# One matrix per system in place of attention and inverse, factors stored with the systems, and other groups of tiles

## What is computed

```
A0   = tril(-(k_beta @ k.T) * L, -1)
A    = inverse(eye - A0)                 # unit lower triangular, 37 x 37
v_new = A @ (v * beta)
attn = tril((k @ k.T) * L)               # diagonal included
o    = attn @ v_new
out  = h + o @ W_read.T
```

## Time and profile before

| | |
|---|---|
| median of 3 runs | 774.7 us (774.45 to 776.15) |
| the profiled execution | 774.87 us, span 773.1 us |
| TensorE busy | 691.6 us (89%) |
| VectorE busy | 419.6 us (54%) |
| ScalarE busy | 246.4 us (32%) |
| GpSimd busy | 292.1 us (38%) |
| mean granted TensorE clock | 0.945 |

### The profile page before, as it was taken

One profiled execution on the slowest core, in us unless ns is written; L12 is line 12 of the kernel. 1 busy time (PEld: TensorE's weight loads), 2 busy tenths in 40 slices (PEclk: granted clock), 3 DMA queues, 4 the chain that ended last, 5 costly groups with the idle time before them and its releaser, 6 DMA issues.

```text
span 773.1 us, 13815 instructions
## 1 busy us (share of the span) xinstructions
PE 691.6 (89%) x4632; PEld 518.9 (67%) x4632; DVE 419.6 (54%) x1120; ACT 246.4 (32%) x679; POOL 292.1 (38%) x483
## 2 busy tenths in 40 slices
PE   5899999999997689999999689497999999999994
PEld 3567776676765445999998567374667676766763
DVE  2466677777665466334389999457233323333331
ACT  0122333333333114344444246261122223232231
POOL 2334454544444100255576687360222322222221
PEclk9899999999998779999999899796799999999998
DMA  8311001111100000000101327598211111111110
GB/s 292 137 37 37 20 25 31 37 37 37 37 1 2 1 1 2 1 8 6 40 8 36 41 44 290 210 361 306 56 40 43 49 54 47 58 42 56 47 35 14
DMA packets 25070, 50.73 MB, mean 66 GB/s; under 512 B 15611, under 2 KB 15741, under 8 KB 24363
## 3 DMA queue, kind: packets, MB, share of 16 engines
q1 hardware_dynamic: 21387, 35.36, 14.4%
q0 software_dynamic: 3328, 10.23, 4.4%
q10 hardware_dynamic: 288, 4.27, 1.4%
HBM read 39.99 MB, written 9.86 MB: 64 GB/s over the span
## 4 chain that ended last, share of the span: by engine, by line
PE 45%; DVE 7%; issue 4%; POOL 3%; ACT 0%; POOLq 0%; DVEq 0%; ACTq 0%
PE psum L1199 12%; PE psum L1175 12%; PE psum L1396 4%; PE psum L1408 4%; PE psum L1188 3%; PE psum L1442 2%; DVE work L1750 2%; PE psum L1376 1%; DVE arena_w L1757 1%; PE psum L1386 1%; PE psum L1018 1%; PE psum L1418 1%; POOL work L1909 1%; PE psum L1448 1%; POOL work L1898 1%
## 5 line engine op out<-in xcount | busy, mean ns | idle before, releaser
L1272 ACT ACTIVATE work<-psum,cst 128x128 f32<-128x128 f32 x208 | 56.5, 383 | 144.2 <-PE psum L1188 144.2
L1175 PE MATMUL psum<-arena_w,work 128*128 x208 | 93.7, 593 | 1.0 <-DVE work L1226 1.0
L1199 PE MATMUL psum<-arena_w,work 128*128 x416 | 94.2, 379 | 0.4 <-ACT work L1272 0.4
L1137 POOL DMA_INDIRECT out<-work,row_i x26 | 25.7, 988 | 158.2 <-DVE work L1248 158.2
L1199 PEld LDWEIGHTS psum<-arena_w,work 128*128 128x128 f32 x416 | 77.1, 190 | 10.5 <-issue 1.1
L1235 DVE COPY work<-psum 128x512 f32<-128x512 f32 x52 | 36.0, 692 | 67.5 <-PE psum L1175 67.5
L347 PE MATMUL psum<-arena_w 128*111 128x256 f32 x264 | 63.3, 392 | 4.9 <-DMA arena_w<-in_pack 4.9
L712 POOL TENSOR_TENSOR arena_w<-arena_w,work 101x592 f32<-101x592 f32 x33 | 39.5, 1198 | 71.6 <-DVE work L578 71.6
L1175 PEld LDWEIGHTS psum<-arena_w,work 128*128 128x128 f32 x208 | 37.5, 190 | 38.6 <-issue 38.6
L347 PEld LDWEIGHTS psum<-arena_w 128*111 128x111 f32 x264 | 46.1, 181 | 19.2 <-issue 9.6
L703 POOL TENSOR_TENSOR arena_w<-arena_w 128x296 f32<-128x296 f32 x66 | 44.0, 689 | 21.2 <-DVE arena_w L546 21.2
(11 more groups left out here) (224 smaller groups left out, 1377.6 us busy)
## 6 DMA issues: line engine op xcount, KB each, us to landing
arena_w<-in_w SPq DMA_DIRECT2D x2, 4096.0 KB, 12.7
arena_w<-in_x SPq DMA_DIRECT2D x22, 333.0 KB, 2.9
x_rows<-tokens SPq DMA_DIRECT2D x22, 192.0 KB, 4.0
arena_w<-in_pack ACTq DMA_DIRECT2D x1, 2442.0 KB, 10.8
cst<-in_packc ACTq DMA_DIRECT2D x1, 1727.0 KB, 14.8
arena_w<-in_pack SPq DMA_DIRECT2D x1, 818.5 KB, 7.1
arena_w<-in_pack SPq DMA_DIRECT2D x2, 384.0 KB, 4.3
arena_w<-n_rows SPq DMA_DIRECT2D x8, 85.6 KB, 3.1
```

The costliest lines, as they stand in the source:

```text
L1175: mm = nc.tensor.matmul(bank[2 * j + f][:, :], xgt[j][:, k * 128:(k + 1) * 128], arena_w1[:, bass.ds(expert * (2 * FF) + (k * FF + f * 512 ...
L1199: mm = nc.tensor.matmul(bank[7][:, 0:D], ht[j][:, g * 128:(g + 1) * 128], arena_w2[:, bass.ds(expert * (FC * D) + g * D, D)], start=(g == ...
L1272: nc.scalar.activation(ht[j][:, g * 128:(g + 1) * 128], bank[4 + f][:, k * 128:(k + 1) * 128], ACT.Gelu, bias=cst[:, bass.ds(expert * FC + ...
```

## The change

1. **One matrix.** `attn @ A` is computed in one piece. With the factors 1/beta stored with each system, it follows from the inverse by a scaling of its columns and an addition on its diagonal. So the mask of line 1696, `attn_t`, `solve_values`, `copy_solved`, `scale_first` and `add_first` go, and the two heads of `read_out` accumulate in one half bank.
2. **Factors with the systems.** A row of `n_rows` has 39 elements instead of 37. `factors(i)` on VectorE writes the two more, per pair, behind the pair's second mask; `store_systems` waits for them too. `substitution` ends with a product over the whole inverse and two additions on its band; `own_factors` on GpSimd prepares these.
3. **Groups** of pairs (0 to 4), (5 to 8) and (9, 10): 2, 2 and 6 sets, 19, 19 and 7 columns.
4. **Moves.** The identity columns are made in turns 0 to 2; `keep_logits` is a copy on ScalarE, and the bias is added once in `route`; the epsilon goes to GpSimd; in GpSimd's turn the powers of the rows come first and the strengths are made for a pair; the last group's systems lie in another part of the memory.

The diff, cut to its core:

```diff
-GROUPS = ((0, 5), (5, 8), (8, PAIRS))
+GROUPS = ((0, 5), (5, 9), (9, PAIRS))
+NW = TOK + 2
...
-    n_rows = nc.dram_tensor("n_rows", (H1, NT * R, TOK), F32).ap()
+    n_rows = nc.dram_tensor("n_rows", (H1, NT * R, NW), F32).ap()
...
                 def store_systems(t):
                     sp.wait_ge(nk_ready, t + 1)
+                    sp.wait_ge(factors_ready, 2 * (t // 2 + 1))
...
                 def load_systems(g):
...
-                    if g == LAST:
-                        sp.wait_ge(z1_done, PAIRS)
...
                 def attend(t):
...
-                    pe.wait_ge(vn_out, t + 1)
+                    pe.wait_ge(a_block, t + 1)
                     free(pe, o_out, t - 1)
                     for h in range(H1):
-                        a = (t * H1 + h) * R
-                        mm = nc.tensor.matmul(bank[2 + t % 2][:, h * R:(h + 1) * R], vn[t % 2][:, h * 128:(h + 1) * 128],
-                                              attn_t[:, a:a + R], start=True, stop=True)
+                        mm = nc.tensor.matmul(bank[t % 2][:, h * R:(h + 1) * R], x_half(t)[:, h * 128:(h + 1) * 128],
+                                              ab[t % 2][:, h * R:(h + 1) * R], start=True, stop=True)
...
-                pe.wait_ge(y_added, PAIRS)
-                read_out(0)
-                attend(1)
                 for t in range(2, NT + 5):
-                    solve_values(t)
+                    attend(t)
+                    turn_outputs(t - 5)
                     read_out(t - 1)
-                    turn_outputs(t - 5)
-                    attend(t)
                     router_logits(t - 5)
...
                 for t in range(2, NT + 5):
+                    copy_attended(t)
+                    copy_turned(t - 5)
                     normalise_outputs(t - 4)
-                    copy_solved(t)
-                    copy_turned(t - 5)
-                    scale_first(t - 1)
-                    copy_attended(t)
+                    keep_logits(t - 5)
...
                     dve.wait_ge(g_done, t + 1)
-                    nc.vector.tensor_tensor(attn_t[:, t * H1 * R:(t + 1) * H1 * R], bank[7][0:R, 0:H1 * R], lt, ALU.mult)
                     free(dve, nk_ready, t - 1)
...
-                    nc.vector.engine_nop().then_inc(solved[g], 1)
+                    nc.vector.tensor_tensor(x, x, n[:, :, TOK + 1].unsqueeze(1).broadcast_to([used, cols, TOK]),
+                                            ALU.mult).then_inc(scaled[g], 1)
+                    dve.wait_ge(scaled[g], 1)
+                    dve.wait_ge(factored[g], 1)
...
+                    nc.vector.tensor_tensor(band, band, own[0:used, 0:TOK - 1].rearrange("p (c k) -> p c k", k=sets),
+                                            ALU.add).then_inc(solved[g], 1)
...
                     dve.wait_ge(r_done, t + 1)
-                    dve.wait_ge(inverted, t // 2 + 1)
-                    dve.wait_ge(half_added, t + 1)
-                    nc.vector.scalar_tensor_tensor(h, bank[4 + j][0:R, D:2 * D], inv_all[:, t * H1 + 1:t * H1 + 2], h,
-                                                   ALU.mult, ALU.add).then_inc(added, 1)
+                    dve.wait_ge(summed, t // 2 + 1)
+                    nc.vector.tensor_tensor(h, h, bank[2 + j][0:R, 0:D], ALU.add).then_inc(added, 1)
                     dve.wait_ge(added, t + 1)
                     free(dve, powered2, t - 1)
                     nc.vector.bn_stats(st2[j][:, 0:6], h).then_inc(stat2, 1)
...
+                def factors(i):
...
+                    nc.vector.reciprocal(to[:, :, :, TOK], beta[:, cols].rearrange("p (b h) -> p b h", b=2)
+                                         ).then_inc(factors_ready, 1)
+                    dve.wait_ge(factors_ready, 2 * i + 1)
+                    nc.vector.scalar_tensor_tensor(to[:, :, :, TOK + 1], sn[:, cols].rearrange("p (b h) -> p b h", b=2), 0.5,
+                                                   to[:, :, :, TOK], ALU.mult, ALU.subtract).then_inc(factors_ready, 1)
...
                     decay_products(i - 2, 1)
+                    factors(i - 2)
                     if i - 3 in ends:
                         queue.append(substitution(ends[i - 3]))
                     advance(SLOTS[2])
...
                 for i in range(-1, PAIRS + 2):
-                    strengths(i - 2, 0)
+                    power_rows(i - 1)
+                    strengths(i - 2)
                     fold(i - 2, 0)
-                    power_rows(i - 1)
-                    strengths(i - 2, 1)
+                    fold(i - 2, 1)
                     add_rows(i - 1)
-                    fold(i - 2, 1)
...
                 for t in range(NT + 2):
-                    add_first(t - 1)
                     spread_inverses(t + 2)
                     power_outputs(t - 2)
+                    if t == 4:
+                        own_factors(LAST)
```

More of the change, by code:

```diff
@@ L146, in build @@
         lg0 = carve_1b(NT * E0, R)
+        carve_2 = carver(arena_w1)
+        for g in range(1, len(GROUPS) - 1):
+            solve_at[g] = [carve_2(w) for w in (TOK * NW, TOK * COLS[g], TOK, TOK)]
         zeros = arena_w2[:, W2S - RW // 2:W2S]
@@ L913, in build @@
             nf = [fc(H1 * R, R) for _ in range(2)]
-            nkb = [fc(H1 * TOK, R) for _ in range(NB)]
+            nk_all = fc(NB * H1 * NW, R)
+            nkb = [nk_all[:, b * H1 * NW:(b + 1) * H1 * NW] for b in range(NB)]
             junk = fc(2 * D, R)
-            th, beta, strength, ss, ssf = (fc(NT * H1, R) for _ in range(5))
+            th, beta, strength, sn, ss, ssf = (fc(NT * H1, R) for _ in range(6))
             st1, ve1 = fc(16, R), fc(8, R)
@@ L1762, in substitution @@
                         dve.wait_ge(chain[which], steps[which])
-                    nc.vector.engine_nop().then_inc(solved[g], 1)
+                    nc.vector.tensor_tensor(x, x, n[:, :, TOK + 1].unsqueeze(1).broadcast_to([used, cols, TOK]),
+                                            ALU.mult).then_inc(scaled[g], 1)
+                    dve.wait_ge(scaled[g], 1)
+                    dve.wait_ge(factored[g], 1)
+                    band = rows_x[0:used, 0:(cols - 1) * (TOK + sets)].rearrange("p (c i) -> p c i", c=cols - 1)[:, :, 0:sets]
+                    nc.vector.tensor_tensor(band, band, own[0:used, 0:TOK - 1].rearrange("p (c k) -> p c k", k=sets),
+                                            ALU.add).then_inc(solved[g], 1)
+                    corner = rows_x[0:used, cols * TOK - 1:cols * TOK]
+                    nc.vector.tensor_tensor(corner, corner, own[0:used, TOK - 1:TOK], ALU.add).then_inc(solved[g], 1)
                 queue = []
@@ L1912, in _ @@
                 load_with = {t: t0 for g in range(len(GROUPS)) for t0, t1 in loads_of(g) for t in range(t0, t1)}
+                ends = {GROUPS[g][1] - 1: g for g in range(len(GROUPS))}
                 for i in range(-1, PAIRS + 2):
-                    strengths(i - 2, 0)
+                    power_rows(i - 1)
+                    strengths(i - 2)
                     fold(i - 2, 0)
-                    power_rows(i - 1)
-                    strengths(i - 2, 1)
+                    fold(i - 2, 1)
                     add_rows(i - 1)
-                    fold(i - 2, 1)
                     if i == PAIRS:
@@ L1992, in lay_out @@
     p["lag"] = np.where(same & (lag > 0), lag, 0)
-    p["keep"] = -1.0 * (same & (lag > 0))
-    p["lag_t"] = np.where(same.T & (lag.T >= 0), lag.T, 0)
-    p["keep_t"] = same.T & (lag.T >= 0)
+    p["keep"] = -0.5 * (same & (lag > 0))
     p["col_no"] = np.zeros((128, sum(COLS)))
```

186 lines of the change are left out of this document (83 added, 103 removed).

## The result

The changed kernel takes 798.3 us (median of four runs, 789.25 to 800.36), the kernel before on the same chip 774.8 (774.45 to 776.15). The ratio is 1.0276, with a 95% interval of 1.0223 to 1.033. So it is slower, as forecast, and by 23.5 us where 17.0 were forecast; 798.3 stands at the upper end of the predicted range, nearer to rival B's 797 than to the forecast's 791.7. The four runs are not alike: three took 797.93 to 800.36 with a mean granted clock of 0.908 or 0.909, the fourth 789.25 with 0.927. The profiled execution of after took 800.36 us with a span of 798.6 and a mean granted clock of 0.908.

What follows compares the result with a forecast made beforehand. VectorE was taken to set the pace from about 418 us. Group two solved at 479.4 and the last at 512.5 put line 1070 at 551.9 against 534.92, +17.0; 774.7 + 17.0 = 791.7 us, range 783 to 798.

Steps and rivals of the forecast that it cites:

- rival B: More of the same: contended steps, a longer second store or longer waits after gaps, +5 to +7 us, 797; chance .10.
- the second group is what costs: VectorE's second substitution starts later and costs 4.8 more, so it is solved at 479.4 against 462.40.
- the first group's tail: New product and two band additions ending the first substitution on VectorE, priced at 1.2 us.
- The two waits for masks: In turn 12 VectorE idles 4.8 us before pair 10's mask, and the second mask waits about .5 more.
- nothing covers it: Tiles 0 to 9 are through before group two is solved; tile 10 goes on at 487.4.
- Rival C: Shorter tiles and removed masks pay for the larger second group, solved about 464: -6.2 us, 768.5; chance .07.
- the last group solved at 512.5: VectorE's last substitution, resumed at 489.1 with tiles 9 to 15 between, ends at 512.5 against 492.13.
- small waits for TensorE: VectorE's waits during the last group, as TensorE restarts after a gap: 1.2 us, ends 0 and 3.
- which path is last: Of two paths to line 1070, row stores finish at 551.8 and the tiles are ready at 548.8; stores are last.
- the six-tile drain: Six tiles and drain before routing, 27.35 us before, 18.6 after; routing starts at 540.0.
- The ring: Small transfers wait for the big one ahead in the queue; the 8 MB land 1.0 before the last group's store.
- Rival A: VectorE not stopped behind tile 8; the last group's store waits for weights landing at 511.5: +10.6, 785.3; chance .17.

Runs made afterwards that it cites:

- Experiment 2: The kernel before with only the new groups of the change: 793.96 us, ratio 1.0269.
- experiment 5: The changed kernel with idle TensorE products filling both gaps, 13 ahead of tile 10 and 16 ahead of tile 18: 787.8 us, ratio 1.0161.
- experiment 9: The changed kernel with the old groups (five, three and three pairs) and 17 idle TensorE products ahead of tile 16: 773.4 us, ratio 0.9975.
- experiment 11: The kernel before with 12 idle TensorE products in its one gap, ahead of tile 16, nothing of the change: 774.4 us, ratio 0.9987.
- Experiment 4: The changed kernel with the last substitution run to its end at tile step 10, in the gap: 788.4 us, ratio 1.0173.
- experiments 4 and 12: Experiment 4, and one matrix, old groups, 15 idle products, first weights behind the last group's store and load, second behind row stores: 787.0 us, ratio 1.0155.
- experiment 1: The changed kernel with the old groups of five, three and three pairs: 781.3 us, ratio 1.008.
- experiments 6 and 7: Changed kernel, old groups, 14 idle products ahead of tile 16: 777.3 us; the same with the second weights' first 4 MB behind row stores: 777.8 us.
- experiment 3: The changed kernel with 26 idle TensorE products ahead of tile 10 and 34 ahead of tile 18: 805.7 us, ratio 1.0403.

## Why the prediction was right, and where not

**Right: the second group is what costs.** Group two was forecast solved at 479.4 and its store goes out at 480.10; its products and reductions took 13.47 + 10.97 = 24.4 (24.3 forecast), the last group's 7.07 + 6.18 = 13.25 (12.8). Experiment 2 shows that this one edit by itself costs 19.2 us. That 480.10 is so near is partly luck, since the parts inside had errors that cancel. The start came at 438.36 instead of 435.4; 1.7 of these 3.0 us are the first group's tail, 1.60 + 1.16 + .15 = 2.9 where 1.2 was priced. The two waits for masks were 3.18 + 2.52 = 5.7 for 4.8 + .5. Only eight tiles, 0 to 7, come before the end, and at 1.0 each: 8.0 where nine were priced at 10.35 (the addition of tile 8 stands at 481.92). And neighbouring rows overlap: from 440.28 to 478.36, without the waits, masks and tiles, 23.3 us pass for the 24.4 of busy time, so the sum of busy times was 1 us too long.

**Right: nothing covers it.** The second group's store to load took 485.48 - 480.10 = 5.4 for 6.0, which makes up for the .7 that it was late. GpSimd went on with tile 10 at 487.50 (487.4 forecast), VectorE was idle 7.13 (7.3), line 1343 was issued at 488.40 (488.2). Rival C, that four tiles fewer and the lighter stage pay for it, needed a store at about 464.

**Wrong in size: the last group solved at 512.5.** It was 518.54. The failed term is "1.2 for small waits for TensorE, which restarts after a gap; ends 0 and 3": these waits were 8.2 us. I took TensorE's tile as 2.57 - .51 = 2.06 from the earlier trace rows, which are rows at full clock, and by this kernel's rows it takes 3.7 at 0.50. The trace of before had shown the low clock too, behind its own gap from 499.75 to 504. At 1.00 (experiment 5) there are no such waits up to the last step, and the group is solved at 508.73: 20.3 us after VectorE's step at 488.43, where 23.4 were forecast and 29.1 measured. So the forecast's 512.5 fell between two clocks, neither of which it named, and that 791.7 lies between 787.8 and 798.3 is luck.

**Rival B.** It asked for one of three causes and +5 to +7 us. Slower steps did not come (24.4 for 24.3), nor did the longer store (5.4, not 7.35). The longer waits after a gap did, 8.2 for 1.2. The measured time is therefore mostly B's, by a cause that B names only by its effect.

**Wrong: which path is last.** I had the stores of rows last at 551.9 and the tiles' path ready at 548.8. The stores were done at 555.16 and line 1063 ran at 558.78 without waiting for them: the six-tile drain took 549.97 - 526.08 = 23.9 for 18.6, again by the clock. At full clock the stores are last, as forecast, at 545.99 (experiment 5), 29.0 after line 1346 for 29.7.

**Not in the sum.** Line 1063 came 558.78 - 534.92 = 23.9 later, the profiled execution ended 25.5 later. The 1.6 between lie behind it: the 44 products of line 1010 took 9.63 for 7.89 before.

**The bill.** With the medians: new groups in the old kernel +19.2; one matrix on top of that +4.3, to 798.3. With the gaps filled the sum is 787.8 - 775.5 = +12.3, of which the groups make 787.8 - 773.4 = 14.4 (experiments 5 and 9) and the one matrix -2.1 (experiment 9 against the kernel before; -1.0 against experiment 11). Filling the gaps gives back 10.5 us by the medians of two chips and 8.9 by the ratios, in which the run of 789.25 pulls the changed kernel down; so the clock costs some 9 to 10 of the 23.5 us.

**The ring.** Experiment 4 shows what the trace of before could only suggest: a store behind the 8 MB is done when these land. The Trainium skill ("DMA: Bandwidth & Descriptors", Queues, rings and completion order) has it that on each DMA engine descriptors are consumed in ring order; experiments 4 and 12 agree (512.8 for a store issued at 494.76, and 36.87 us for the issues of 44 rows that took 27.27 in experiment 9). They do not part that order from the held-up issuing: in experiment 4 the last of the twelve goes out only at 507.3. In the changed kernel it costs nothing, since the last group is solved after the landing. Rival A was therefore right on the mechanism and wrong on VectorE's order.

**Open.** What brings TensorE's clock back is not settled. In the traces the old tile loop (five products, 2.57 us per tile) had it back 3 to 4.3 us after each gap of before and of experiment 2. The new one (four, 1.9 us at full clock) stayed at 0.50 for 29.6 us in after (488.1 to 517.7) and for 22 us in experiment 1, where the clock came back at 525.4, just behind the last tile that has an `attend`. Both loops keep TensorE busy 10.00 of 10. But the loop alone does not decide: in experiment 4 the new one had the clock back after 3.5 us behind its first gap and not behind its second, and the run of 789.25 has a higher mean clock with the same program as the others. The runs show further that a filled gap prevents the low clock, and that 2.6 to 3.0 us of gap left (experiments 6 and 7) are enough to lose it in some runs.

## What to carry to other kernels

Price a stage behind a gap at both clocks: take the granted clock of that window, not the best tile, and see whether the low clock would then be on the path; look at more than one run, since the clock can come back in one and not in the next. Idle products that fill the gap gave back some 9 to 10 us here; they must be sized from their measured length, as experiment 3 shows. Moving work between groups of a serial chain is judged by what covers each group's latency; and a large transfer should be placed in the ring only where no small one that someone waits for comes behind it.

## What was not expected of the hardware

- The clock stayed at 0.50 from 480 to about 541, although TensorE was busy without a break from 488.1 to 517.7, and again from 526.7 on after a second gap of 8.98 us; in the kernel before, it was back about 4 us after the gap, in experiment 4 after 3.5.
- A VectorE operation of 36 elements took 1.16 us in one place (line 1738 at 431.60) and 0.20 in two others; one of 703 took 1.60 and 1.42, where 648 elements took .83.
- SyncE's own issuing of 12 small DMAs took 12.88 us behind an 8 MB transfer (8.5 of it for the eleventh), 4.46 without one.
- A float32 product of 128x512 is two instructions and takes 0.87 us at full clock.
